# Third layer of a four-layer graph network: GpSimd takes all the remainders, ScalarE weights five pairs of seven, and VectorE compares four groups of five

## The reference, cut to what matters

```python
Wr, Wc = Wh[row], Wh[col]                      # one row per edge and end
dot = sum(Wr * Wc); nr, nc = norms of Wr, Wc
sim = dot / maximum(nr * nc, EPS)
base = adj_v * softplus(...) * (row != col)
prop_pos = segment_sum((base *  relu( sim))[:, None] * Wc, row)
prop_neg = segment_sum((base * -relu(-sim))[:, None] * Wc, row)
out = scale * (coeff[0] * prop_pos + coeff[1] * prop_neg + coeff[2] * Wh)
```

## Time and profile before

| | |
|---|---|
| median of three runs | 3910.35 us |
| the profiled execution | 3914.72 us, of which its span 3913.0 us |
| granted TensorE clock over the span | 0.915 |
| third layer, first to last product (L1271) | 1886.1 to 2880.2 us, 343 groups |
| busy share over the whole span | TensorE 78%, VectorE 83%, ScalarE 55%, GpSimd 34% |

### The profile page before, as it was taken

The page is one execution under the profiler, slowest core; times in us unless marked ns, Lnnn a source line. Parts: engine busy times, 40 slices in busy tenths (PEclk is TensorE's granted clock), DMA queues, the critical chain, the costliest instruction groups (busy, mean ns, idle before and its releaser), DMA issues.

```text
span 3913.0 us, 125366 instructions
## 1 busy us (share of the span) xinstructions
PE 3052.9 (78%) x50473; PEld 2725.6 (70%) x50473; DVE 3231.2 (83%) x6988; ACT 2164.1 (55%) x5734; POOL 1346.9 (34%) x1644
## 2 busy tenths in 40 slices
PE   0288888888888779899677778777757778788786
PEld 0167777777777679899677777777746777777775
DVE  7599999999999733233899999999967889989997
ACT  5323333333333410001778878788756888888887
POOL 2000000000000000000487778778753555555554
PEclk9999999999999989999899999999877888888887
DMA  8156666666666779898676777777628888888884
GB/s 210 54 168 205 209 206 209 208 209 208 212 213 211 233 297 361 342 327 301 229 245 225 236 236 243 224 241 241 229 92 273 256 251 256 257 258 255 253 255 141
DMA packets 655939, 907.64 MB, mean 232 GB/s; under 512 B 363978, under 2 KB 587883, under 8 KB 636412
## 3 DMA queue, kind: packets, MB, share of 16 engines
q1 hardware_dynamic: 633240, 800.64, 63.7%
q10 hardware_dynamic: 19763, 94.38, 6.4%
q0 software_dynamic: 2352, 4.52, 0.6%
HBM read 651.96 MB, written 247.40 MB: 230 GB/s over the span
## 4 chain that ended last, share of the span: by engine, by line
DVE 39%; PE 30%; DMA 11%; ACT 9%; issue 7%; SPq 2%; POOL 1%; ACTq 0%; DVEq 0%; POOLq 0%
PE ps L626 7%; PE ps L964 7%; DVE U L754 5%; DMA U<-AD 3%; DMA A<-ROWS 3%; DVE EDG L777 3%; DMA T<-ROWS 3%; DVE U L1271 2%; PE ps L1178 2%; DVE EDG L1300 2%; PE ps L1190 2%; PE ps L1171 2%; DVE U L1632 2%; DVE U L1263 2%; SPq L1396 2%
## 5 line engine op out<-in xcount | busy, mean ns | idle before, releaser
L542 ACT ACTIVATE U<-ps 128x512 bf16<-128x512 f32 (+1 forms) x637 | 359.1, 573 | 666.3 <-PE ps L638 666.0
L1148 POOL TENSOR_TENSOR EDG<-U,edge 128x256 f32<-128x256 f32 x343 | 243.3, 710 | 852.5 <-DVE edge L1296 733.1
L1464 ACT ACTIVATE U<-U,T 128x65 f32<-128x65 f32 x1806 | 459.7, 339 | 107.5 <-PE ps L1552 94.2
L1178 PE MATMUL ps<-U 128*128 128x65 bf16 x7203 | 304.2, 200 | 209.3 <-DVE edge L1274 207.5
L964 PE MATMUL ps<-U 128*128 128x192 bf16 x4802 | 421.2, 249 | 37.6 <-DVE U L1041 19.2
L487 POOL DMA_INDIRECT U<-REC,nod x49 | 45.2, 922 | 1164.7 <-PE ps L582 1041.5
L964 PEld LDWEIGHTS ps<-U 128*128 128x128 bf16 x4802 | 405.7, 99 | 46.6 <-DMA U<-AD 23.2
L1178 PEld LDWEIGHTS ps<-U 128*128 128x128 bf16 x7203 | 265.6, 102 | 231.0 <-DVE edge L1274 228.6
L777 DVE TENSOR_TENSOR EDG<-edge,EDG 128x896 bf16<-128x896 bf16 x686 | 406.6, 618 | 8.9 <-DMA OSD<-EDG 7.5
L1490 POOL TENSOR_TENSOR U<-U 128x455 f32<-128x455 f32 x258 | 275.7, 1069 | 329.7 <-DVE U L1632 329.7
L651 PE MATMUL ps<-EDG,U 128*128 128x193 bf16 x2401 | 310.8, 251 | 62.5 <-ACT U L542 41.3
(11 more groups left out here) (303 smaller groups left out, 7407.2 us busy)
## 6 DMA issues: line engine op xcount, KB each, us to landing
U<-AD SPq DMA_DIRECT2D x98, 1568.0 KB, 8.6
U<-ROWS SPq DMA_DIRECT2D x343, 448.0 KB, 4.4
OND<-EDG SPq DMA_DIRECT2D x343, 224.0 KB, 2.3
OSD<-EDG SPq DMA_DIRECT2D x343, 224.0 KB, 3.2
AD<-U ACTq DMA_DIRECT2D x49, 1568.0 KB, 6.4
EDG<-ROWS SPq DMA_DIRECT2D x343, 224.0 KB, 4.9
U<-OND SPq DMA_DIRECT2D x303, 224.0 KB, 5.2
EDG<-OSD SPq DMA_DIRECT2D x189, 224.0 KB, 4.7
```

The lines of the kernel that those rows point to most:

```text
L542: ev4.by(act.activation(prow[i % NPW][:, P * g:P * (g + m)], ps[4 + gg % 2][:, 0:P * m], ACT.Copy))
L1178: ins = pe.matmul(ps[2 + h][:, 65 * k:65 * k + 65], rw[r][:, 2 * P * k:2 * P * k + P], Ws[:, j, s_, 0:65], start=(s_ == 0), stop=(s_ == 2))
L1464: ins = act.activation(V4[k % NV][:, 0, c, :], H[d % 3][:, s, :], ACT.Copy, scale=a4[d % 2][:, s:s + 1])
```

## The change

Four things are changed in the third layer. GpSimd makes the first remainder for all seven pairs in one instruction of 128 x 448 and waits for ScalarE's values (`vm_a`) before it; VectorE's part (L1300) is gone. ScalarE weights five pairs of seven (`KA = 5`), GpSimd two, so its value instruction is 128 x 128. ScalarE compares every fifth group and VectorE the other four. The coefficient is written as `(c0 - c1) * max(sim, 0) + c1 * sim`, one instruction fewer; the difference is made once, early in the program (`sc[:, 19:20]`).

```diff
             dv.by(dve.tensor_scalar(sc[:, 16:19], sc[:, 8:11], sc[:, 15:16], None, ALU.mult))
+            dve.wait_ge(dv.at, dv.n)
+            dv.by(dve.tensor_tensor(sc[:, 19:20], sc[:, 16:17], sc[:, 17:18], ALU.subtract))
...
-        KA = 3
+        KA = 5
...
-        rem3, low3, rem3p = on(hid, NB), on(relu, NB), on(outp, NB)
+        rem3, low3 = on(outp, NB), on(relu, NB)
...
-            return n // 3 + 1
+            return n // 5 + 1
...
                     pool.wait_ge(vm_p.at, m + 1)
-                    rem3p.by(pool.tensor_tensor(V3[m % 4][:, 1, KA:G, :], V3[m % 4][:, 0, KA:G, :], S3[m % 4][:, 0, KA:G, :], ALU.subtract))
+                    pool.wait_ge(vm_a.at, m + 1)
+                    rem3.by(pool.tensor_tensor(V3[m % 4][:, 1, :, :], V3[m % 4][:, 0, :, :], S3[m % 4][:, 0, :, :], ALU.subtract))
                 m = n - 10
                 if 0 <= m < NG:
-                    pool.wait_ge(rem3p.at, rem3p.o + m + 1)
                     pool.wait_ge(rem3.at, rem3.o + m + 1)
...
-                if n % 3 == 0:
+                if n % 5 == 0:
                     r = n % NR
...
-                dvf.by(dve.tensor_scalar(a, b_, 0.0, sc[:, 16:17], ALU.max, ALU.mult))
-                dvf.by(dve.tensor_scalar(c_, b_, 0.0, sc[:, 17:18], ALU.min, ALU.mult))
+                dvf.by(dve.tensor_scalar(a, b_, 0.0, sc[:, 19:20], ALU.max, ALU.mult))
                 dve.wait_ge(dvf.at, dvf.n)
-                dvf.by(dve.tensor_tensor(a, a, c_, ALU.add))
+                dvf.by(dve.scalar_tensor_tensor(a, b_, sc[:, 17:18], a, ALU.mult, ALU.add))
...
-            def remainder(m):
-                dve.wait_ge(vm_a.at, m + 1)
-                rem3.by(dve.tensor_tensor(V3[m % 4][:, 1, 0:KA, :], V3[m % 4][:, 0, 0:KA, :], S3[m % 4][:, 0, 0:KA, :], ALU.subtract))
-
             for n in range(4):
                 columns(n)
             for n in range(NLAST):
-                if 0 <= n - 9 < NG:
-                    remainder(n - 9)
```

More of the change, by code:

```diff
@@ L1162, in ends @@
                 r, h, j, i0 = n % NR, n % 2, n // NQ, G * (n % NQ)
-                if n % 3:
+                if n % 5:
                     pe.wait_ge(hot_d.at, n + 1 - by_act(n))
```

## The result

The changed kernel takes 3890.69 us (median of five runs, 3886.59 to 3897.21), against 3910.35 us before; the ratio is 0.9952, 95% interval [0.9936, 0.9967]. That is 20 us gained where 123 had been forecast, and outside the range of 3748 to 3855 us. The direction was right, the size was not.

The account below looks back on a forecast made before the run. VectorE was taken to set the 2.951 us pitch. Its 2.48 us plus 4% loss gave 2.58, saving 107 us over 288 groups and 17 over 46 others: 3914.7 - 124 = 3791, median 3787 us, range 3748 to 3855 us.

Parts of the forecast that it names:

- What bounds the kernel: Third layer before the change: VectorE, busy 96%, sets the pitch of 2.951 us per group; the other engines follow.
- GpSimd: GpSimd's time per group after the change, with losses to VectorE's compares: 2.38 to 2.44 us.
- ScalarE: ScalarE's time per group with two more values and fewer compares: 2.30 to 2.51 us.
- TensorE: TensorE's matmuls do nothing else than before: 1.92 us per group at the full clock.
- DMA: Bytes per group stay; share about 0.82 at a pitch near 2.6 us, costed at nothing.
- VectorE: VectorE's time per group without L1300, with more compares, longer holds, shorter coefficient: 2.895 falls to 2.48 us.
- The pitch: Time per group in the third layer: VectorE's 2.48 plus the earlier 4% loss gives 2.58 us, 0.37 less.
- The rival of ScalarE's burst: ScalarE's five values plus compare outrun the rings every fifth group: pitch 2.77 us, 3850 us; chance 0.18.
- the 0.1 named as its mark: Sign of the burst: GpSimd's remainder waits for ScalarE's values by more than 0.1 us per group.
- full exclusion: VectorE's compares and small instructions stop GpSimd for their whole length: pitch 2.84 us, 3873 us; chance 0.11.
- The argument against exclusion: Same count for the kernel before gives 2.98 us, over its 2.951 pitch; GpSimd's worst loss is 0.43 to 0.46, not 0.675.
- the sign named for exclusion: In the third layer GpSimd's instructions would lose over 0.5 us per group.

Follow-up runs that it names:

- remainders, ScalarE as before: Changed kernel with ScalarE's old share put back (three pairs of seven weighted, every third group compared), GpSimd still making all remainders: 3859.84 us, ratio 0.9870.
- port experiment: Separate program, not the network: disputed VectorE and GpSimd instructions, 40 in a row, apart and together; compare pitch 0.60 us alone, 1.47 beside GpSimd.
- both mechanisms cut away: Changed kernel with GpSimd's first remainder on one pair of seven from the fifth group and ScalarE's compare on 2 of 1792 columns (work left out): 3744.17 us.

## Why the prediction was wrong, by its own steps

*What bounds the kernel* and the direction were right: VectorE set the pitch, and taking its remainder away made the kernel faster.

*GpSimd*: 2.38 to 2.44 us forecast. Measured 2.881 less its waits of (96.0 + 35.1) / 295 = 0.44, that is 2.44; the value instruction 0.39 us, the remainder 0.92. Right. *ScalarE*: 2.30 to 2.51; busy 714 / 295 = 2.42. Right. *TensorE* and *DMA*: right; the clock was 0.94, no DMA shows among the waits, and TensorE's for VectorE was 96.6 / 295 = 0.33 us (waits, 1950 to 2800 us):

```profile
PE ps L1180 <- DVE edge L1276: 96.6, 75, 4.6
```

*VectorE* is the first step that failed. "I take 0.25 us lost each, 0.06 more per group" was too small for the compare, and for the small instructions nothing was taken. Forecast 2.48, measured 2.881 - 22.0 / 295 = 2.81. Of the 0.33 between them these rows give 0.30:

- the compare: 254.0 / 295 = 0.86 us per group, forecast 162.6 / 288 + 0.10 + 0.06 = 0.72: 0.14;
- the coefficient's six instructions: 0.46 us per group, after 0.36 for seven before (750 us window), where 0.34 was forecast: 0.12;
- the addition of a finished block: 0.09 per group after 0.05: 0.04.

One instruction of the coefficient was indeed gone, but those left over were held longer. The last of them shows it best. In the kernel before it took 246 ns in the mean and never more than 254, for at this point GpSimd often stood still, waiting for this very coefficient (55.7 us). In the changed kernel that wait is down to 8.6 us, GpSimd is at work instead, and the same instruction (L1297) takes 620 ns. The kernel before, 1950 to 2700 us:

```profile
L1296 DVE TENSOR_TENSOR edge<-edge,E 128x49 f32<-128x49 f32 x36 | 8.9, 246 | 1.5 <-DVE edge L1291 0.2
```

The error lay in pricing the hold by GpSimd's share of the time. The table has no such law: with GpSimd busy 635 of 750 us the compare lasts 1077 ns, with 711 it lasts 947 ("remainders, ScalarE as before"). The port experiment has the upper bound, 0.87 us per compare and 0.94 per small instruction, with GpSimd never idle; the changed kernel's compare loses 1072 - 669 = 403 ns, about half of that. I had named a hold of 658 ns, 0.39 us more per group, as the compare's worst and then chosen near the lower end. What sets the hold between these bounds is not settled.

*The pitch* is the second step: "The same loss on 2.48 gives 2.58" took engines within 0.15 us of each other to lose no more than one engine alone. The rival of ScalarE's burst was real: 0.32 us per group of GpSimd's wait for it (95.7 / 295), past the 0.1 named as its mark. Splitting the burst gives 33 us back, leaving its instructions out 51. The step also counts something twice. The 2.48 starts from 2.895, the pitch less VectorE's waits, and so the gaps between its dependent instructions are in it already; the loss from 2.895 to 2.951 is 2%, while the 4% that was added has the gaps in it again. With 2% the forecast pitch would have been 2.53, and the miss larger: this slip brought the number nearer by luck. The sum 2.48 itself was sound for a VectorE meeting no more than the assumed hold: with both mechanisms cut away the pitch was 2.47.

*The rivals.* The 3850 us of the burst and the 3873 us of full exclusion were each on the right side of the forecast, and neither alone reaches the measured 3891; the experiments show both at work. The argument against exclusion, that the same count for the kernel before exceeds its pitch, was right about the size of one hold on GpSimd (0.37 us in the port experiment, not 0.675) and missed that VectorE is the one that pays. So the sign named for exclusion, GpSimd's instructions losing over 0.5 us per group, did not show: they lost (501 - 389) + (984 - 925) + (1042 - 925) = 0.29 us. The Trainium skill, page "SBUF — State Buffer", section "Who interferes with whom", says that whichever engine starts first keeps the shared port pair for the whole instruction and the other blocks fully, and that a VectorE instruction with at most one input in SBUF does not contend, outside its two-port modes. The runs agree in the main: a pitch of 0.12 us becomes 1.06, and with one operand in PSUM neither engine slows the other. But an alternating pair of compare and GpSimd instruction takes 1.46 us where the sum of the two pitches, 0.60 + 1.09, would be 1.69, so some 0.2 us of each pair still overlap.

Of the 104 us that did not come, the two edits that only take away holds and split the burst give back 95 in number. Not all of it is what was missing: with its operands in PSUM the coefficient takes 0.24 us per group (750 us window), less than the 0.34 forecast, so a part of the 95 comes from holds that the kernel before had too. How the loss divides between the two mechanisms is not settled; each edit works only as far as the other mechanism lets it.

## What to carry to other kernels

- Before moving work from VectorE to GpSimd, price what GpSimd does to VectorE's instructions with two SBUF inputs and to its bf16 compares. GpSimd's mean share does not give it. One whole GpSimd instruction for each is the upper bound (0.87 us for the compare); the kernels here paid 0.24 to 0.44 us of it. Count the small instructions too; an operand in PSUM takes them out of it (620 ns became 238).
- When a change brings several engines to within some per cent of each other, look at the longest burst of each, not only at its mean, and try to spread it over iterations (33 us here).
- Where two mechanisms hold the same pitch, a small gain from one edit does not mean that its mechanism is small: here two edits gave 27 and 33 us apart and 95 together.

## What the runs showed of the hardware that was not expected

- A VectorE instruction of 49 elements with both inputs in SBUF had a pitch of 1.06 us in place of 0.12 beside a GpSimd that was never idle, while GpSimd's 40 instructions took 43.48 us with and without it. Against the compare of 1792 elements GpSimd lost 0.37 us and VectorE 0.87; with GpSimd instructions of 128 elements in place of 448 GpSimd lost 0.38 and VectorE 0.19.
- A remainder of 320 elements took 603 ns in the mean beside a GpSimd that was busy 63% of the time and had shorter instructions, one of 192 elements 625 ns beside one busy 79%.
- GpSimd's f32 subtraction of 448 elements has a pitch of 1.09 us when each waits on the fourth before it, in the port experiment, and a pitch of 0.89 in the network (2407.69 to 2408.58).
